# Attention scores and weighted sums by whole rows over all eight PSUM banks, with the second normalisation in another order behind the sums

## The reference

```python
x = x + conv(ln_c(x), Wq, Wk, Wv, rq, rk, rv, Gq, Gk, Gv1, Gv2)
t = tokens(x)
t = t + ffn(ln_t(t), W, V, gamma, beta)

def conv(x, ...):                       # x: (16, 32, 32, 32) = n, c, i, j
    q, k, v = (einsum('oc,ncij->noij', W_, x) for W_ in (Wq, Wk, Wv))
    weight = softmax(einsum('ncij,nchj->nihj', q, k) / d
                     + Gq * einsum('ncij,chi->nihj', q, rq) / d
                     + Gk * einsum('ncij,chi->nihj', k, rk) / d, axis=3)
    return einsum('nihj,nchj->ncij', weight, Gv1 * v) + einsum('nihj,chi->ncij', weight, Gv2 * rv)

def ffn(x, W, V, gamma, beta):          # batch norm of x @ W.T, then a scan over 1024 tokens
    wx = batchnorm(x @ W.T) * gamma + beta
    y_t = sigmoid(wx_t + y_(t-1) @ V.T)
```

## Time and profile before

| what | value |
|---|---|
| device time, median of 3 runs | 143.99 us |
| the runs | 145.23, 140.79, 143.99 us |
| the profiled execution | 142.81 us |
| its span | 141.0 us |
| busy share PE, DVE, ACT, POOL | 70%, 66%, 52%, 46% |

### The profile page before, as it was taken

How to read it: one execution, slowest core, us unless ns; L and a number is a source line. 1 busy time by engine, 2 the same in 40 slices (tenths; PEclk the granted TensorE clock), 3 DMA queues, 4 the chain that set the end, 5 groups by cost and what they waited for, 6 DMA issues and landing times.

```text
span 141.0 us, 4751 instructions
## 1 busy us (share of the span) xinstructions
PE 99.0 (70%) x2058; PEld 68.5 (49%) x2058; DVE 92.6 (66%) x143; ACT 73.8 (52%) x157; POOL 64.6 (46%) x71
## 2 busy tenths in 40 slices
PE   0496996968689989888995444078269888999200
PEld 0222331357578888767885443032023248999100
DVE  5899487000003879947730298989997678888992
ACT  7956886726464035994321026143612389999300
POOL 8997717982000186979000079964620000006930
PEclk9999999999999999999999999559955999999985
DMA  4891499989700000133663000000000000000667
GB/s 147 261 270 15 96 209 209 205 195 239 192 10 5 5 7 5 42 97 91 153 155 83 1 7 5 0 0 0 0 0 5 0 0 0 0 7 1 202 187 205
DMA packets 9825, 11.67 MB, mean 83 GB/s; under 512 B 2828, under 2 KB 6924, under 8 KB 9804
## 3 DMA queue, kind: packets, MB, share of 16 engines
q1 hardware_dynamic: 9228, 10.31, 28.8%
q10 hardware_dynamic: 576, 1.05, 3.0%
HBM read 2.97 MB, written 2.10 MB: 36 GB/s over the span
## 4 chain that ended last, share of the span: by engine, by line
PE 24%; DVE 17%; ACT 17%; issue 12%; POOL 10%; DMA 9%; SPq 9%; ACTq 0%; POOLq 0%; DVEq 0%
PE ps L1008 9%; DMA gates<-in_L_conv_Gk_dram 5%; PE ps L1072 5%; ACT warm L676 5%; PE ps L1051 4%; POOL y_tile L432 4%; SPq L282 4%; DMA v_tile<-u_tile 4%; DVE xin L347 4%; PE ps L1061 3%; DVE y_tile L353 3%; POOL y_tile L176 2%; POOL y_tile L438 2%; ACT v_tile L676 2%; ACT rel_tile L526 2%
## 5 line engine op out<-in xcount | busy, mean ns | idle before, releaser
L353 POOL TENSOR_TENSOR y_tile<-xin,u_tile 128x256 f32<-128x256 f32 (+1 forms) x7 | 7.1, 1049 | 25.6 <-DVE xin L347 25.6
L1072 PE MATMUL ps<-rel_tile,w_bd 128*128 128x512 f32 x16 | 12.1, 902 | 8.8 <-DVE rel_tile L832 8.8
L1008 PE MATMUL ps<-spread,v_tile 128*32 128x64 f32 x512 | 13.2, 257 | 3.3 <-issue 1.9
L409 POOL TENSOR_TENSOR att_tile<-att_tile,soft 128x1024 f32<-128x1024 f32 x4 | 7.7, 1942 | 16.1 <-DVE soft L767 16.1
L1008 PEld LDWEIGHTS ps<-spread,v_tile 128*32 128x32 f32 x512 | 12.3, 201 | 3.8 <-issue 3.0
L613 ACT ACTIVATE square<-y_tile 128x512 f32<-128x512 f32 x8 | 5.0, 629 | 16.9 <-POOL y_tile L432 16.9
L1061 PE MATMUL ps<-spread,v_tile 128*32 128x64 f32 x512 | 8.9, 223 | 6.8 <-issue 6.8
L750 DVE STREAM_TRANSPOSE rv_t<-att_tile 128x1024 f32<-128x1024 f32 x1 | 1.3, 1251 | 17.6 <-ACT att_tile L573 17.6
L905 DVE TENSOR_SCALAR ps<-att_tile,bnv 128x512 f32<-128x512 f32 x15 | 11.0, 808 | 1.6 <-ACT warm L676 1.6
L1061 PEld LDWEIGHTS ps<-spread,v_tile 128*32 128x32 f32 x512 | 8.0, 109 | 7.6 <-issue 7.6
L1072 PEld LDWEIGHTS ps<-rel_tile,w_bd 128*128 128x128 f32 x16 | 4.2, 283 | 14.8 <-DVE rel_tile L832 12.6
(11 more groups left out here) (108 smaller groups left out, 240.0 us busy)
## 6 DMA issues: line engine op xcount, KB each, us to landing
out_dram<-y_tile SPq DMA_DIRECT2D x8, 256.0 KB, 2.4
xin<-in_x_dram SPq DMA_DIRECT2D x3, 512.0 KB, 4.9
spread<-att_tile SPq DMA_DIRECT2D x12, 128.0 KB, 2.4
v_tile<-u_tile SPq DMA_DIRECT2D x12, 128.0 KB, 2.4
spread<-rel_tile SPq DMA_DIRECT2D x24, 64.0 KB, 2.2
xin<-in_x_dram SPq DMA_DIRECT2D x2, 256.0 KB, 2.8
spread<-u_tile SPq DMA_DIRECT2D x4, 128.0 KB, 2.3
v_tile<-u_tile ACTq DMA_DIRECT2D x4, 128.0 KB, 4.3
```

The costliest lines, as they stand in the source:

```text
L353: return eng.tensor_tensor(result[:, :, rows, :], back[:, at:at + P * k].rearrange("p (q i j) -> p q i j", q=Q, i=k), x2[:, :, rows, :], A ...
L409: nc.gpsimd.tensor_tensor(att_m[:, n, :, :], att_m[:, n, :, :], soft[:, 0, n, :].unsqueeze(2).broadcast_to([P, C, C]), ALU.subtract).then_ ...
L1008: return nc.tensor.matmul(ps[group(g), first + j // 8, at:at + Q * HALF].rearrange("p (q i) -> p q i", q=Q), u_by_q[:, g, :, j], y_bd[:, : ...
L1072: nc.tensor.matmul(bank(WX_BANK[k % 2]), w_bd[:, 1, :], by_row(tokens, k), start=True, stop=True).then_inc(S["wx_product"], 1)
```

## The change

Scores: all 32 columns of i in one product (128 moving columns in place of 64), half as many products, in all eight banks; so the first `score_add` waits for the whole, the last columns wait for `rel_out`, and TensorE goes on to the values only after all four adds. Weighted sums: the same, one series over all eight banks, which waits for `att_in0` and `att_in1` together; every `residual` waits for the end of it. The second normalisation mixes the halves (`centre(4)` after `scale(0)`, `residual(4)` after `t_sum2(0)`, and so on), all four first `project_wx` wait for the last residual, and 26 more blank products stand ahead of them and in their midst. In the first part `rel_out` moves from ACT to DVE, the last `turn_y` from POOL to ACT, one `keep_warm` product is added, and some steps of the first layer norm change places. On POOL `weigh(1)` and `shift_scores(2)` change places.

```diff
@@ score banks, SP @@
-        SCORE_A, SCORE_B = 2, 0
-        WSUM_BANK = [0, 4]
...
-                if q < 3:
-                    sp.wait_ge(S["y_turned_act"], q + 1)
-                else:
-                    sp.wait_ge(S["y_turned_pool"], 1)
+                sp.wait_ge(S["y_turned_act"], q + 1)
...
-                sp.wait_ge(S["score_b_high"], 1)
+                sp.wait_ge(S["score_product"], 1)
@@ POOL @@
             weigh(0)
+            shift_scores(2)
             weigh(1)
-            shift_scores(2)
             shift_scores(3)
...
             scale(0)
+            centre(4)
             scale(1)
+            centre(5)
             scale(2)
+            centre(6)
             scale(3)
-            centre(4)
-            centre(5)
             scale(4)
-            centre(6)
             scale(5)
@@ ACT @@
+            value_out(2)
             turn_weights(0)
-            value_out(2)
             value_out(3)
-            turn_weights(1)
             value_out(4)
             score_exp(2)
             value_out(5)
+            turn_weights(1)
             value_out(6)
+            value_out(7)
             score_exp(3)
-            value_out(7)
             turn_weights(2)
@@ DVE @@
+            def rel_out(n):
+                rows = slice(ROWS * (n % 4), ROWS * (n % 4 + 1))
+                dve.wait_ge(S["rel_product"], n + 1)
+                nc.vector.tensor_copy(rel[:, n // 4, :, rows, :], side_bank(n).rearrange("p (i q j) -> p q i j", i=ROWS, q=Q)
+                                      ).then_inc(S["rel_ready"], 1)
...
             def score_add(n):
-                first = SCORE_A if n < 2 else SCORE_B
-                if n < 2:
-                    dve.wait_ge(S["score_a"], 1)
-                else:
-                    dve.wait_ge(S["score_b_low"], 1)
-                    dve.wait_ge(S["score_b_high"], 1)
+                dve.wait_ge(S["score_product"], 1)
...
             def residual(k):
                 half, q = k // Q, k % Q
                 dve.wait_ge(S["relv_ready"], 4 * (half + 1))
-                dve.wait_ge(S["wsum_product"], half + 1)
+                dve.wait_ge(S["wsum_product"], 1)
@@ TensorE @@
+            def scores():
+                for j in range(C):
+                    at = Q * C * (j % 4)
+                    if j // 4 in SIDE and j % 4 == 0:
+                        pe.wait_ge(S["rel_ready"], PIECES4 - 1 + SIDE.index(j // 4))
                     for g in range(G):
-                        ins = score(half, j, g)
+                        ins = nc.tensor.matmul(ps[group(g), j // 4, at:at + Q * C].rearrange("p (q i) -> p q i", q=Q),
+                                               u_by_q[:, g, :, j], y_bd[:, :, g, j // RUN, :, j % RUN],
+                                               start=True, stop=True)
...
-            keep_warm(2, 3)
+            keep_warm(2, 4)
...
-            scores(0, range(C)).then_inc(S["score_a"], 1)
-            scores(1, range(HALF)).then_inc(S["score_b_low"], 1)
-            pe.wait_ge(S["score_sum"], 2)
-            scores(1, range(HALF, C)).then_inc(S["score_b_high"], 1)
+            scores().then_inc(S["score_product"], 1)
+            pe.wait_ge(S["score_sum"], CHUNKS)
...
             pe.wait_ge(S["att_in0"], 16 * Q * G)
-            weighted_sums(0, range(C)).then_inc(S["wsum_product"], 1)
             pe.wait_ge(S["att_in1"], 16 * Q * G)
             pe.wait_ge(S["first_beta"], 1)
-            weighted_sums(1, range(0, HALF))
+            weighted_sums(range(0, 24))
             pe.wait_ge(S["relv_ready"], PIECES4)
-            weighted_sums(1, range(HALF, C)).then_inc(S["wsum_product"], 1)
+            weighted_sums(range(24, C)).then_inc(S["wsum_product"], 1)
...
+            pe.wait_ge(S["blank_set"], 1)
+            pe.wait_ge(S["x2_ready"], UNITS)
+            blank_banks([0, 1] + [WARM_BANK] * 16)
             project_wx(0)
             project_wx(1)
-            pe.wait_ge(S["blank_set"], 1)
-            blank_banks([0, 1])
             project_wx(2)
             project_wx(3)
-            pe.wait_ge(S["x2_ready"], UNITS)
-            blank_banks([4, 5, 6, 7])
+            blank_banks([4, 5, 6, 7] + [WARM_BANK] * 10)
             project_wx(4)
```

More of the change, by code:

```diff
@@ L497, in u_half @@
                 nc.scalar.copy(u_tile[:, IMG * q + BANK * k:IMG * q + BANK * (k + 1)], bank(SIDE[k])).then_inc(S["u_half"], 1)
[L499 to L505, removed]
             def score_exp(n):
@@ L535, in _ @@
             ln_square(2)
+            turn_y(0)
+            ln_std(2)
+            u_half(0, 0)
+            u_half(0, 1)
             spread_out(0, 4)
             spread_out(1, 3)
[L538 to L541, removed]
+            turn_y(1)
             act.wait_ge(S["turned"], 1)
@@ L545, in _ @@
             ln_square(3)
[L546 to L549, removed]
             ln_square(4)
@@ L557, in _ @@
             u_half(2, 1)
+            turn_y(3)
             act.wait_ge(S["y_in1"], 16 * G)
@@ L563, in _ @@
                 act.dma_start(v_tile[group(3), IMG * g:IMG * (g + 1)], u_tile[group(g), IMG * 3:IMG * 4]).then_inc(S["u_in"], 16)
[L564 to L569, removed]
-            rel_out(6)
-            rel_out(7)
             act.wait_ge(S["rv_in"], 16 * G)
@@ L748, in _ @@
             ln_out(4)
+            def rel_out(n):
[3 more added lines that the diff above has]
+                                      ).then_inc(S["rel_ready"], 1)
+            for n in range(PIECES4):
+                rel_out(n)
             dve.wait_ge(S["rv_scaled"], 1)
@@ L784, in _ @@
             score_max(1)
+            score_add(2)
+            score_add(3)
             weight_sum(0)
-            score_add(2)
+            score_max(2)
             weight_sum(1)
-            score_max(2)
-            score_add(3)
             score_max(3)
             weight_sum(2)
+            relv_out(0)
+            relv_out(1)
             weight_sum(3)
-            for n in range(PIECES4):
+            for n in range(2, PIECES4):
                 relv_out(n)
@@ L798, in residual @@
                 dve.wait_ge(S["relv_ready"], 4 * (half + 1))
-                dve.wait_ge(S["wsum_product"], half + 1)
-                first = WSUM_BANK[half]
+                dve.wait_ge(S["wsum_product"], 1)
                 nc.vector.tensor_tensor(unit(x2, k),
-                                        ps[:, first:first + 4, :].rearrange("p b (j q i) -> p q i (b j)", q=Q, i=HALF)[:, q],
+                                        ps[:, :, :].rearrange("p b (j q i) -> p q i (b j)", q=Q, i=C)[:, q, HALF * half:HALF * (half + 1)],
                                         unit(x2, k), ALU.add).then_inc(S["x2_ready"], 1)
@@ L842, in _ @@
             t_sum2(0)
+            residual(4)
             t_sum2(1)
             t_rstd(0)
+            residual(5)
             t_sum2(2)
             t_rstd(1)
+            residual(6)
             t_sum2(3)
             t_rstd(2)
+            residual(7)
             t_rstd(3)
-            residual(4)
-            residual(5)
             t_turn(0)
@@ L859, in _ @@
             t_rstd(5)
-            residual(6)
-            residual(7)
             bn_part(0)
@@ L1003, in project_u @@
                     ins.then_inc(S["u_product"], 1)
-            def score(half, j, g):
-                first = SCORE_B if half else SCORE_A
-                at = Q * HALF * (j % 8)
-                return nc.tensor.matmul(ps[group(g), first + j // 8, at:at + Q * HALF].rearrange("p (q i) -> p q i", q=Q),
-                                        u_by_q[:, g, :, j], y_bd[:, :, g, j // RUN, HALF * half:HALF * (half + 1), j % RUN],
-                                        start=True, stop=True)
-            def scores(half, js):
-                for j in js:
+            def scores():
[3 more added lines that the diff above has]
+                        pe.wait_ge(S["rel_ready"], PIECES4 - 1 + SIDE.index(j // 4))
                     for g in range(G):
-                        ins = score(half, j, g)
+                        ins = nc.tensor.matmul(ps[group(g), j // 4, at:at + Q * C].rearrange("p (q i) -> p q i", q=Q),
+                                               u_by_q[:, g, :, j], y_bd[:, :, g, j // RUN, :, j % RUN],
+                                               start=True, stop=True)
                 return ins
@@ L1054, in relative_values, with weighted_sums @@
                 ins.then_inc(S["relv_product"], 1)
-            def weighted_sums(half, rows):
-                first = WSUM_BANK[half]
-                for j in rows:
-                    at = Q * HALF * (j % 8)
+            def weighted_sums(js):
+                for j in js:
+                    at = Q * C * (j % 4)
                     for g in range(G):
-                        ins = nc.tensor.matmul(ps[group(g), first + j // 8, at:at + Q * HALF].rearrange("p (q i) -> p q i", q=Q),
-                                               v_t[:, j, g, :], att_bd[:, :, g, half, j // RUN, :, j % RUN],
```

(2 more changed lines are left out.)

38 lines of the change are left out of this document (18 added, 20 removed).

## The result

The changed kernel takes 152.09 us (median of 4 runs; before, beside it, 143.34): 1.07 times the time of before, 95% interval 1.048 to 1.092. The profiled execution takes 150.83, its span is 149.0.

| mark | before | forecast | after |
|---|---|---|---|
| first add of scores | 46.31 | 47.05 | 46.69 |
| SP's first weight DMA, behind the first add | 10.97 | 14.2 | 13.40 |
| start of the sums, behind that DMA | half 0 alone | 20.8 | 18.89 |
| first residual, behind the start of the sums | 8.20 | 10.05 | 8.77 |
| first residual | 80.09 | 92.1 | 87.75 |

A forecast was written before the change was run, and what follows sets the result against it. Bound by the chain through scores, SP's 24 weight DMAs, sums and second normalisation, with the two halves overlapping from 71.89. Forecast: 142.81 + 12.0 (first residual) + 1.5 (to last statistics) = 156.3 us, range 153 to 159, chance 0.60.

The forecast's parts named there:

- signs of being wrong: Prediction is wrong if the sums begin before 77, or the clock is full in the values and in the sums.
- Parts 1 and 2: Up to first add: 0.7 later, at 47.05; from there to first turned weights: 14.2 instead of 10.97, values at half clock.
- Part 3: Weights' way back: SP's 24 DMAs stay at 20.8, but the sums need the last, starting at 82.05 against 71.89.
- Rival 4: SP's queue: the 24 DMAs go out closer; at 0.35 us each 146.0, from 0.39 not slower; chance 0.03.
- Part 4: Weighted sums: 7.74 at full speed plus 2.2 for a lowered clock; first residual at 92.1 instead of 80.09, +12.0.
- Part 5: First residual to last statistics: TensorE's queue sets it, 32.9 instead of 31.4, +1.5.
- The main term: First residual: +12.0, since lost overlap of the halves costs more than the vanished fetch gaps, about 7 us, save.
- Rival 1: Clock stays at 2.4 GHz in all three TensorE waits: 149.7 us; chance 0.17.
- Rival 2: The wait ahead of the scores lowers the clock too: +2.0 to 2.95, about 159; chance 0.16 together with rival 3.
- Rival 3: Issue gaps in the sums stay at 0.9 to 1.85 per 128 records: up to +4.5, 160.8; 0.16 with rival 2.

The follow-up runs named there:

- the part alone: Kernel before with only whole-row weighted sums and the new order of the second normalisation, with its blank products: 150.68 us beside 143.81, ratio 1.057.
- The parts alone: Kernel before plus one piece each: early steps, 143.55 us; whole-row scores with softmax lists, 145.90; whole-row sums with new normalisation order, 150.68.

## Why the prediction was right

The direction and the main mechanism held: the first residual has to wait for all weights and all sums, and that costs more than the wide products save. None of the signs of being wrong came: the sums begin at 78.98 and not before 77, and the clock was at half in the values, though full in the sums. The sizes of parts 3 and 4 were too large.

**Parts 1 and 2 held.** Wide scores end no earlier than half 0 did (8.05 us for 256 records, 7.74 forecast); the shift of 0.5 by the added warm product is not seen (38.60 against 38.61). The four adds leave TensorE idle and the values start at half clock. The first turned weights came 0.8 sooner than forecast. About 0.2 of it is the clock, which rose 3.2 us into the values where the forecast's pieces come out at about 3.5; the rest is in the steps behind the third piece, 1.2 us in place of 1.8.

**Part 3, the term that was most off.** SP took 17.41 for its 24 DMAs, not 19.14, so the last landed about 2 us sooner than I had from the earlier trace rows. Rival 4 went this way, but by 0.07 us a DMA, far from the 0.39 us a DMA at which it would have decided. That the last weight DMA releases the sums was shown by the part alone, where TensorE waits for it by name; in the changed kernel its landing at about 78.9 fits their start at 78.98.

**Part 4, mis-sized in the changed kernel.** I had put 2.2 us on a clock that is down. It stayed up: the fourth chunk of weights came late enough to keep TensorE at the relative values until 76.5, and only 2.46 us of idle time were left. (The clock was at half for 3 us inside these relative values, 5.45 us for 128 records; they still ended ahead of the last weight DMA.) In the part alone the idle time was 5.03, the clock fell, and the sums took 10.1, the forecast number. So the mechanism is there and its condition was misjudged. What the condition is stays open: with 2 and 4 blank products an idle time of 3.28 ahead of the sums left the clock up (256 records in 7.83), with the narrow sums one of 3.20 did not.

**Part 5, right in size, wrong in what ends last.** TensorE's queue sets the first four projections, but not the last: DVE's transposes do, behind a square root that waits on ACT, which adds 0.52 us. It came to 31.7 and not 32.9 because the blank products start 12.75 behind the first residual (13.5 forecast) and take 6.46 and 3.19 (6.9 and 3.6 forecast).

**The main term.** Lost overlap was forecast at +12.0 on the first residual and measured at +7.7; parts 3 and 4 explain 3.2 of the difference. The parts alone cost about 0, 2.8 and 7 to 8 us, which sum to 10 to 11 beside a whole of 9 to 10. Undoing the sums alone gives back 2 to 3 by the times and 4.5 by the traces from the first add on. That late scores and late sums hide each other in part is therefore argued and not shown.

**Rivals.** Rival 1 held for one of the three waits, that ahead of the sums; the clock fell ahead of the values and again ahead of the blank products. Rival 2 is real and belongs to the first part of the change: of the six profiled executions with that part, five have some 3 us of half clock in the first scores, and only that of the changed kernel itself has not; the eight without it have full clock there. Wide scores take 9.5 us with it and 8.05 without. How often the changed kernel pays it in its other executions is not on record, so differences of some 1.5 us between such kernels stay open. Rival 3 is refuted: wide records ran without the gaps.

## What to carry to other kernels

Before merging two half-size stages into one, price the work that the second half hid, not the instructions saved: here TensorE gained some 7 us twice, and the time rose by 7%. An idle stretch of TensorE can be paid again by what comes after it, at half clock, and products that only keep the clock up gave back here about what they cost. When a part is undone and little comes back, do not read the time alone: compare the traces stage by stage from a common mark, since a stage that the edit does not touch may have run slower in those executions.

## What the runs showed of the hardware

TensorE's clock fell to half at very different idle times: 1.3 us after the last sums before (a burst of 0.33 us behind a gap of 1.29), 3.2 us after the last relative values with the sums and the order alone, 4 us after the last scores in the changed kernel, while 2.46 us ahead of its sums left it up, and 3.28 us with 2 and 4 blank products. It rose 3.0, 3.2 and 5.9 us after work began. The scores stage of the changed kernel took 8.05 us in one execution and 9.5 in four of variants that do not touch it, by the clock in its first half.

A run of narrow products came at about 128 records in 3.5 to 4.0 us, with a gap of 0.75 to 1.95 us between the packets of instructions in the sums (0.2 to 0.9 in the scores, whose products run slower), also where nothing else moved on the DMA queues; twice as wide products had none.
